# Sparse experts: first layer's bias moved to VectorE, second's bias product over 128 rows, a wait for the expert's own weights, first weights fetched in the layer before

## The chip, the cores and the metric

One core of one Trainium2 chip runs the whole kernel as one program. The metric is the device time of one execution in microseconds (us). "The span" is the time from the first to the last instruction of the profiled execution.

## The reference, cut to what matters

Four layers work on 8 x 512 tokens of width 256, each followed by a normalisation: attention, a quantized two-layer network, linear attention with decay, and at last a latent attention with eight sparse experts. The change is in the last of them:

```python
mla_out = ao @ o_w + o_b
probs = softmax(mla_out @ router_w + router_b)
topw, topi = top_k(probs, 2)
topw = topw / (topw.sum(-1) + 1e-8)
combine = sum(one_hot(topi, 8) * topw[..., None], axis=-2)
h1 = gelu(einsum('bsd,edf->ebsf', mla_out, w1) + b1)   # w1: 8 x 256 x 512
h2 = einsum('ebsf,efd->ebsd', h1, w2) + b2             # w2: 8 x 512 x 256
x = layernorm(hs + hs + 0.3 * einsum('bse,ebsd->bsd', combine, h2))
```

## The kernel before

The program runs one block after another: `attention` ("soft"), `quantized_ffn`, `attention` ("decay"), `latent_attention` ("mla") and `sparse_experts` ("moe"). Within a block the engines have programs of their own, in an order written out by hand, tied by semaphores. SyncE (SP) issues the plain DMAs, GpSimd (POOL) the indirect ones.

**`latent_attention`** scatters each token's vector twice, sorted by expert, into the DRAM tensor `by_expert`, and leaves the number of rows of each expert in `counts`. SyncE first loads weights and small tables, waits for `ones_ready`, and then `spread((0, 0))` copies yh and yl into `stack` and `pad` as soon as they are made. ScalarE writes exponentials into `pt`, four groups deep, one for each t; TensorE reads them in its step "A".

**`sparse_experts`, start.** SyncE issues six small loads (among them `blank`, 1 MB), then 16 weight pieces of 512 KB (w1 and w2 of each expert by turns) through the four buffers of `raw`, a piece from the fifth on only when an older one has been split. VectorE makes `table` (for each of 72 tiles its row in `by_expert` and its expert's number) in 14 steps, out of `counts`. ScalarE makes the high part of each piece (`hi_split`), VectorE the low one (`lo_split`, line 1737). When all pieces are issued, SyncE copies the biases' high and low parts, row by row, 16 DMAs, into `bias` [2, 8, 768], and then `blank` behind the experts' regions in `by_expert` (line 1602). After that it fetches the tiles, line 1612.

**Loop over 72 tiles.** Each tile has 128 rows and one expert. A slot works on four tiles at once. TensorE's order in slot s is: transposes of tile s+2 into `ps_x` (line 1661); first layer of tile s+1 into `ps_h` (a 2-row matmul of `ones` with the bias, line 1670, then six of 512 columns, 1672 to 1674); four transposes of g of tile s (1682); second layer of tile s-1 into `ps_y` (a 2-row bias matmul, 1691, then twelve of 256 columns, 1693 to 1695). ScalarE casts x (1792), makes `g` by Gelu straight from `ps_h` (1798) and casts gh (1804). VectorE makes xl (1743), gl (1747) and the weighted answer yo (1755). GpSimd scatters the answer (1819). Line 1652 loads the expert's number of a tile from `table` into a register of TensorE, once for the first and once for the second layer, since the addresses of the weights depend on it. Before the loop TensorE waits for all 16 splits. Two slots ahead, the first eight tiles and the last ones are written out; 56 slots lie in a hardware loop of seven turns with eight slots each.

**End.** For each of 8 batches SyncE loads the two answers of every token (into `w1h`, four batches deep) and x; GpSimd adds the answers (1825); VectorE adds twice x (1768), takes statistics (1771, 1776) and, a batch later, normalises (1762); GpSimd adds EPS (1832) and takes the power -1/2 (1834). SyncE stores the result.

Of the kernel before, what the change touches and what calls it, by code (L numbers as in the profile page):

```python
# [18 lines left out]
F32 = mybir.dt.float32  # L19
# [6 lines left out]
P = 128  # L26
# [925 lines left out]
def latent_attention(nc, const, x_in, sorted_out, counts, w, name):  # L952
# [8 lines left out]
    with ctx:  # L961
# [27 lines left out]
        pt = sb("pt", [P, TT, 4, SEQ])  # L989
# [108 lines left out]
        with nc.Block() as block:  # L1098

            @block.sync  # L1100
            def _(sp):
# [39 lines left out]
                hold(sp, ones_ready, 2)  # L1141
                spread((0, 0))
# [7 lines left out]
            def _(pe):  # L1150
# [4 lines left out]
                def steps(i, run):  # L1155
                    in_misc = [k for k in run if k in bank]
                    for key in run:
# [43 lines left out]
                        elif kind == "A":  # L1201
# [6 lines left out]
                            for s in range(4):  # L1208
                                last = nc.tensor.matmul(ps_a[32 * s:32 * s + 32, 0, :], v[:, t, 4 * a + s, :], pt[:, t, s, :], start=(t == 0), stop=(t == TT - 1), tile_position=(0, 32 * s))
# [177 lines left out]
            def _(act):  # L1387
# [12 lines left out]
                def steps(i, run):  # L1400
                    for key in run:
# [103 lines left out]
def sparse_experts(nc, const, x_in, by_expert, answers, counts, w, x_out, name):  # L1505
# [6 lines left out]
    with ctx:  # L1512
# [5 lines left out]
        RAW = 4  # L1518
        raw = sb("raw", [P, RAW, KD * F])
        bias = sb("bias", [2, E_, F + D], F32R)  # L1520
        ones = sb("ones", [2, P], F32R)
# [7 lines left out]
        table = sb("table", [P, 2, TILES], I32)  # L1529
# [6 lines left out]
        raw_b = xt[:, :, :].rearrange("p k n -> p (k n)")[0:E_, 0:F + D]  # L1536
        hi_b, lo_b = (x[:, :, :, :].rearrange("p a k n -> p (a k n)")[0:E_, 0:F + D] for x in (gh, gl))
        past = g_line[:, 0:TILES * E_].rearrange("p (n e) -> p n e", e=E_)
        over = g_line[:, TILES * E_:TILES * E_ + E_ * (BATCH * SEQ // P)].rearrange("p (e m) -> p e m", e=E_)
        st6, mv, vare, rstd = sb("st6", [P, 2, TT, 6]), sb("mv", [P, 2, TT, 2]), sb("vare", [P, 2, TT, 1]), sb("rstd", [P, 2, TT, 1])  # L1540
        ps_x, ps_h, ps_g, ps_y = (ctx.enter_context(nc.psum_tensor(f"{name}_{n}", [P, 2, F], F32)) for n in ("ps_x", "ps_h", "ps_g", "ps_y"))
        small_in, staged, hi_split, lo_split = sem("small_in"), [sem(f"staged{k}") for k in range(RAW)], sem("hi_split"), sem("lo_split")
        made, bias_split, bias_in, table_step, counted = sem("made"), sem("bias_split"), sem("bias_in"), sem("table_step"), sem("counted")
# [6 lines left out]
        stored = [sem(f"stored{k}") for k in range(4)]  # L1550
        hold = gated_hold(sem("held"))

        pieces = [(e, n) for e in range(E_) for n in range(2)]
# [6 lines left out]
        x_part = lambda b: raw[:, b % RAW, :]  # L1560
        y_part = lambda b, c: w1h[:, 2 * (b % 4) + c, :, :].rearrange("p k n -> p (k n)").bitcast(F32)
        TABLE = 14
# [21 lines left out]
        with nc.Block() as block:  # L1584

            @block.sync
            def _(sp):
                sp.dma_start(raw_b, w["biases"]).then_inc(small_in, 16)
# [3 lines left out]
                for c, (e, n) in enumerate(pieces):  # L1592
                    if c >= RAW:
                        hold(sp, lo_split, c - RAW + 1)
                    src = (w1, w2)[n][e].rearrange("(k p) n -> p k n", p=P)
                    sp.dma_start(piece(e, n)[0].rearrange("p (k n) -> p k n", n=src.shape[2]), src).then_inc(staged[c % RAW], 16)
                hold(sp, bias_split, 2)
                for e in range(E_):
                    for r, part in enumerate((hi_b, lo_b)):
                        sp.dma_start(bias[r:r + 1, e, :].bitcast(F32), part[e:e + 1, :].bitcast(F32)).then_inc(bias_in, 16)  # L1600
# [24 lines left out]
                for b in range(BATCH):  # L1625
                    if b >= 4:
                        hold(sp, stored[b % 4], 16 * (b // 4))
                    for c in range(2):
                        at = (c * BATCH + b) * SEQ
                        sp.dma_start(y_part(b, c).rearrange("p (t d) -> p t d", d=D), answers[at:at + SEQ, :].rearrange(tok, p=P)).then_inc(tile_in[b % 4], 16)  # L1630
                    if b >= RAW:
                        hold(sp, summed, b - RAW + 1)
                        sp.dma_start(x_part(b).rearrange("p (t d) -> p t d", d=D), x_in[b].rearrange(tok, p=P)).then_inc(staged[b % RAW], 16)
                    if b >= 2:
                        hold(sp, normed, TT * (b - 1))
                        sp.dma_start(x_out[b - 2].rearrange(tok, p=P), y_part(b - 2, 0).rearrange("p (t d) -> p t d", d=D)).then_inc(stored[(b - 2) % 4], 16)
# [293 lines left out]
```

## Time and profile before

| | us |
|---|---|
| median of three runs | 3590.7 (3590.26 to 3591.96) |
| profiled execution, its own time | 3593.07 |
| its span | 3590.8 |
| `latent_attention`, from about | 2366 |
| `sparse_experts`, from about | 3121 |
| first transposes of the loop | 3179.7 |
| first load of the end | 3518.4 |

Over the span TensorE (PE) is busy for 84%, its weight loads (PEld) for 59%, VectorE (DVE) for 56%, ScalarE (ACT) for 38%, GpSimd (POOL) for 26%. The granted TensorE clock is 0.931 of full speed in the mean. Times in the rows are us from the start of the span unless marked ns. "q" behind an engine's name means its sequencer, which loads registers, waits, branches and issues while the engine itself may work or stand; TensorE's sequencer is PEldq.

### The profile page before, as it was taken

The numbers are of one execution on the slowest core, as the hardware profiler recorded it, in microseconds if no ns is written. First come the engines' busy times: TensorE is split into PE (matmuls) and PEld (weight loads), VectorE is DVE, ScalarE is ACT, GpSimd is POOL, SyncE is SP. The second block draws the span as 40 slices with busy tenths as digits, with TensorE's granted clock in tenths as the row PEclk, the third lists the DMA queues.
The fourth block names the chain that finished last, engine by engine and source line by source line (L and its number), as shares of the span: only waits on it lengthen the run. The fifth ranks groups of instructions, "written<-read, shape, count | busy, mean of one in ns | idle before, by whom it ended". The sixth has DMA issues, their size and how long they took to land. (4 is left out here: it accounts for less than half of the span.)

```text
span 3590.8 us, 62854 instructions
## 1 busy us (share of the span) xinstructions
PE 3031.4 (84%) x17666; PEld 2116.8 (59%) x17667; DVE 2019.2 (56%) x3902; ACT 1349.6 (38%) x2815; POOL 941.3 (26%) x1262
## 2 busy tenths in 40 slices
PE   5989898998989985877999999969888888359991
PEld 4665666656666655765777777744444444247771
DVE  3656555465646556764666666556666666333334
ACT  3545445354545441222222222215444444233330
POOL 3332332333333311213333333310111111212224
PEclk8999999999999997997999999979999999679995
DMA  1000000000000002111000000022222222241115
GB/s 46 1 14 1 14 1 14 6 9 14 1 13 1 7 8 73 38 64 58 12 12 12 12 12 12 6 56 59 59 59 59 59 60 57 69 139 58 57 54 171
DMA packets 103470, 132.37 MB, mean 37 GB/s; under 512 B 16472, under 2 KB 80088, under 8 KB 102624
## 3 DMA queue, kind: packets, MB, share of 16 engines
q1 hardware_dynamic: 96352, 110.89, 10.4%
q0 software_dynamic: 6912, 18.96, 1.4%
q8 instruction: 101, 1.65, 0.2%
q14 instruction: 105, 0.86, 0.1%
HBM read 64.66 MB, written 36.78 MB: 28 GB/s over the span
## 5 line engine op out<-in xcount | busy, mean ns | idle before, releaser
L612 ACT ACTIVATE soft_probs<-soft_ps_s,soft_mx 128x512 f32<-128x512 f32 x512 | 348.5, 688 | 359.3 <-DVE soft_mx L516 342.6
L1328 DVE TENSOR_REDUCE mla_mx<-mla_ps_s 128x1 f32<-128x512 f32 x512 | 333.7, 685 | 198.0 <-PE mla_ps_s L1188 195.5
L1430 ACT ACTIVATE mla_pt<-mla_ps_t 128x512 f32<-128x512 f32 x512 | 290.9, 600 | 354.7 <-PE mla_ps_t L1200 349.0
L516 DVE TENSOR_REDUCE soft_mx<-soft_ps_s 128x1 f32<-128x512 f32 x512 | 328.3, 684 | 134.0 <-PE soft_ps_s L405 116.2
L416 PEld LDWEIGHTS soft_ps_p<-ident,soft_probs 128*128 128x128 f32 x2048 | 227.5, 143 | 259.2 <-ACT soft_probs L612 57.5
L416 PE MATMUL soft_ps_p<-ident,soft_probs 128*128 128x128 f32 x2048 | 316.7, 286 | 29.7 <-DVE soft_pt L536 23.1
L405 PE MATMUL soft_ps_s<-soft_ks,soft_qs 128*128 128x512 f32 x1024 | 304.9, 422 | 43.0 <-ACT soft_probs L612 32.2
L434 PE MATMUL soft_ps_m<-soft_pt,soft_v 128*64 128x512 f32 x1024 | 268.3, 610 | 1.3 <-DVE soft_v L505 1.3
L1188 PE MATMUL mla_ps_s<-mla_stack,mla_pad 128*128 128x512 f32 x512 | 229.4, 455 | 26.1 <-DVE mla_mx L1328 21.3
L536 DVE COPY soft_pt<-soft_ps_p 128x512 f32<-128x512 f32 x256 | 174.3, 681 | 104.7 <-PE soft_ps_p L416 103.9
L1200 PE MATMUL mla_ps_t<-mla_shifted,mla_pad 128*128 128x512 f32 x512 | 219.2, 430 | 14.1 <-ACT mla_pt L1430 11.7
L405 PEld LDWEIGHTS soft_ps_s<-soft_ks,soft_qs 128*128 128x128 f32 x1024 | 185.1, 196 | 77.4 <-ACT soft_probs L612 37.2
L407 PE MATMUL decay_ps_s<-decay_qs,decay_ks 128*128 128x512 f32 (+3 forms) x1024 | 195.3, 334 | 31.3 <-DVE decay_pt L523 30.5
L498 DVE TENSOR_TENSOR soft_rt<-soft_ps_m,soft_rope 128x1024 f32<-128x1024 f32 (+1 forms) x96 | 100.4, 1046 | 206.9 <-PE soft_ps_m L110 186.9
L523 DVE TENSOR_TENSOR decay_pt<-decay_ps_s,decay_dec 128x512 f32<-128x512 f32 (+3 forms) x512 | 213.7, 482 | 5.4 <-PE decay_ps_s L407 5.4
L619 ACT COPY soft_pt<-soft_ps_p 128x512 f32<-128x512 f32 x256 | 150.9, 589 | 174.5 <-PE soft_ps_p L416 173.6
L407 PEld LDWEIGHTS decay_ps_s<-decay_qs,decay_ks 128*128 128x128 f32 x1024 | 173.3, 199 | 63.8 <-DVE decay_pt L523 42.3
L649 POOL TENSOR_TENSOR decay_rt<-decay_rt 128x256 f32<-128x256 f32 (+1 forms) x192 | 122.6, 660 | 302.9 <-DVE decay_rt L498 302.9
L649 POOL TENSOR_TENSOR soft_rt<-soft_rt 128x256 f32<-128x256 f32 (+1 forms) x192 | 122.2, 657 | 303.3 <-DVE soft_rt L498 303.3
L1188 PEld LDWEIGHTS mla_ps_s<-mla_stack,mla_pad 128*128 128x128 f32 x512 | 100.8, 197 | 163.5 <-DVE mla_mx L1328 79.9
L498 DVE TENSOR_TENSOR decay_rt<-decay_ps_m,decay_rope 128x1024 f32<-128x1024 f32 (+1 forms) x96 | 100.5, 1047 | 126.0 <-POOL decay_st L654 101.5
L313 ACT CAST decay_st<-decay_rt 128x512 fp32r<-128x512 f32 x64 | 39.7, 620 | 334.1 <-POOL decay_rt L649 220.2
(328 smaller groups left out, 6744.7 us busy)
## 6 DMA issues: line engine op xcount, KB each, us to landing
mla_pad<-mla_stack SPq DMA_DIRECT2D x256, 64.0 KB, 2.0
moe_xt<-by_expert SPq DMA_DIRECT2D x72, 129.0 KB, 2.1
mla_stack<-mla_yh SPq DMA_DIRECT2D x128, 64.0 KB, 2.1
moe_raw<-in_L_ffn_w SPq DMA_DIRECT2D x16, 512.0 KB, 5.1
moe_w1h<-answers SPq DMA_DIRECT2D x16, 512.0 KB, 6.2
soft_xc<-in_L_attn_x SPq DMA_DIRECT2D x8, 512.0 KB, 3.9
x<-soft_r SPq DMA_DIRECT2D x32, 128.0 KB, 2.0
ffn_xc<-x SPq DMA_DIRECT2D x8, 512.0 KB, 3.9
```

Source lines behind the costliest of these rows:

```text
L405: last = nc.tensor.matmul(ps_s[:, t, :], qs[:, h, P * t:P * t + P], ks[:, n, g, :], start=(n == 0), stop=(n == 1))
L407: last = nc.tensor.matmul(ps_s[:, t, P * t:SEQ], ks[:, n, g, P * t:P * t + P], qs[:, h, P * t:SEQ], start=(n == 0), stop=(n == 1))
L416: last = nc.tensor.transpose(ps_p[:, c % 2, P * t:P * t + P], probs[:, h % 2, t, P * c:P * c + P], ident[:, :])
L434: last = nc.tensor.matmul(m[HD * s:HD * s + HD, first_q[c]:SEQ], v[:, 1, c, HD * g:HD * g + HD], weights_of(2 * p + s, c), start=(c == 0), ...
L516: op = vv.tensor_reduce(out=mx[:, h, t:t + 1], in_=ps_s[:, t, :], axis=AX.X, op=ALU.max, negate=True)
L523: op = vv.tensor_tensor(weights_of(h, t), ps_s[:, t, P * t:SEQ], dec[:, h, 0:SEQ - P * t], ALU.mult)
L612: op = nc.scalar.activation(probs[:, h % 2, t, :], ps_s[:, t, :], ACT.Exp, bias=mx[:, h, t:t + 1], scale=1.0, accum_out=rs[:, h, t:t + 1])
L649: op = nc.gpsimd.tensor_tensor(half(0, c), half(0, c), half(1, 1 - c), ALU.add)
L1188: last = nc.tensor.matmul(ps_s[:, (4 * t + s + 16 * a) % S_BANKS, :], pad[:, QUADS + a, s, P * t:P * t + P], stack[:, a, :], start=True, s ...
L1200: last = nc.tensor.matmul(ps_t[:, s % 2, :], pad[:, a, s, P * t:P * t + P], shifted[:, a, :], start=True, stop=True)
L1328: op = vv.tensor_reduce(out=mx[:, a, t, s:s + 1], in_=ps_s[:, (16 * a + 4 * t + s) % S_BANKS, :], axis=AX.X, op=ALU.max, negate=True)
L1430: op = nc.scalar.activation(pt[:, t, s, :], ps_t[:, s % 2, :], ACT.Exp, scale=KPH ** -0.5)
```

## The change

- Line 1670, the first bias matmul, goes. `bias_h` holds b1 of all experts in every partition, by one broadcast DMA of 2 MB. VectorE adds it: `g = ps_h + bias_h[expert]`, with a table load of its own for the expert's number. ScalarE's Gelu then works in place on `g`.
- The second bias matmul stays, but over 128 rows: `ones` is 1 in rows 0 and 1 and 0 elsewhere, `bias_y` [128, 8, 256] is cleared by GpSimd and its two first rows loaded by one DMA out of a DRAM copy `bias_parts`, which two DMAs write.
- TensorE doesn't wait for all 16 splits. Before each first layer it loads a third row of `table`, 2 * expert + 2, and waits until `lo_split` has that value. The table takes 16 steps.
- The first four weight pieces are issued by SyncE in `latent_attention`, between its wait for `ones_ready` and `spread((0, 0))`; `raw` is allocated for both layers, and `pt` has two groups instead of four to make room.
- SyncE's order in the start: small loads, pieces 4 to 7, `blank` into `by_expert`, bias parts, pieces 8 to 11, `bias_y` and `bias_h`, pieces 12 to 15, then the fetches, which wait for these DMAs.
- In the end every batch has buffers of its own in w1h and w1l, so that all loads are issued without a wait; ScalarE normalises, `rstd * y + shift_by`, and issues the stores; GpSimd makes shift_by = -mean * rstd in two more operations.

```diff
-        pt = sb("pt", [P, TT, 4, SEQ])
+        pt = sb("pt", [P, 2, 4, SEQ])
...
                 hold(sp, ones_ready, 2)
+                for dst, src, done in pieces_in:
+                    sp.dma_start(dst, src).then_inc(done, 16)
                 spread((0, 0))
...
                             if s == 0:
-                                act.wait_ge(*(pe_s.at(j, "A", a - 1, t) if a else pe_s.at(shift(j, -1), "A", QUADS - 1, t)))
-                            op = nc.scalar.activation(pt[:, t, s, :], ps_t[:, s % 2, :], ACT.Exp, scale=KPH ** -0.5)
+                                u = 4 * a + t - 2
+                                act.wait_ge(*pe_s.at(j if u >= 0 else shift(j, -1), "A", u % 16 // 4, u % 4))
+                            op = nc.scalar.activation(pt[:, t % 2, s, :], ps_t[:, s % 2, :], ACT.Exp, scale=KPH ** -0.5)
...
# sparse_experts, SyncE
+                for c in range(RAW, RAW + 4):
+                    stage(c)
                 hold(sp, small_in, 16 * 6)
                 sp.dma_start(by_expert[...], w["blank"][1].bitcast(F32)).then_inc(bias_in, 16)
+                hold(sp, bias_split, 2)
+                for r, part in enumerate((hi_b, lo_b)):
+                    sp.dma_start(bias_parts[r], part.bitcast(F32)).then_inc(parts_out, 16)
+                for c in range(RAW + 4, len(pieces)):
+                    stage(c)
+                    if c == RAW + 7:
+                        hold(sp, parts_out, 32)
+                        hold(sp, cleared, 1)
+                        sp.dma_start(bias_y[0:2, :, :].bitcast(F32), bias_parts).then_inc(bias_in, 16)
+                        sp.dma_start(bias_h[:, :, :], w["biases"][:, 0:F].partition_broadcast(P)).then_inc(bias_in, 16)
                 hold(sp, tails_in, 16 * E_)
                 hold(sp, table_step, TABLE)
-                hold(sp, bias_in, 16 * (2 * E_ + 1))
+                hold(sp, bias_in, 48)
...
# TensorE
-                pe.wait_ge(lo_split, len(pieces))
-                pe.wait_ge(bias_in, 16 * 2 * E_)
+                pe.wait_ge(bias_in, 48)
...
                         e = expert_of(i, n)
+                        split = pe.value_load(table[0:1, 2, bass.ds(U * i + n, 1)], min_val=2, max_val=2 * E_)
+                        pe.wait_ge(lo_split, split)
                         pe.wait_ge(xl_done, count(i, n) + 1)
...
-                            pe.wait_ge(g_done, count(i, n) - 1)
+                            pe.wait_ge(h_biased, count(i, n) - 1)
-                        nc.tensor.matmul(m, ones[:, :], bias[:, bass.ds(e, 1), 0:F], start=True, stop=False)
...
-                        nc.tensor.matmul(m, ones[:, :], bias[:, bass.ds(e, 1), F:F + D], start=True, stop=False)
+                        nc.tensor.matmul(m, ones[:, :], bias_y[:, bass.ds(e, 1), :], start=True, stop=False)
...
# VectorE, between xl of tile s+2 and gl of tile s
+                    n = s + 1
+                    if inside(i, n):
+                        e = dve.value_load(table[0:1, 1, bass.ds(U * i + n, 1)], min_val=0, max_val=E_ - 1)
+                        dve.wait_ge(h_done, count(i, n) + 1)
+                        if not isinstance(i, int) or U * i + n >= 2:
+                            dve.wait_ge(back, count(i, n) - 1)
+                        vv.tensor_tensor(g[:, n % 2, :], ps_h[:, n % 2, :], bias_h[:, bass.ds(e, 1), :], ALU.add).then_inc(h_biased, 1)
...
# ScalarE
-                        nc.scalar.activation(g[:, n % 2, :], ps_h[:, n % 2, :], ACT.Gelu).then_inc(g_done, 1)
+                        nc.scalar.activation(g[:, n % 2, :], g[:, n % 2, :], ACT.Gelu).then_inc(g_done, 1)
...
+                for b in range(BATCH):
+                    act.wait_ge(rstd_done, b + 1)
+                    for t in range(TT):
+                        nc.scalar.activation(y_part(b, 0)[:, D * t:D * t + D], y_part(b, 1)[:, D * t:D * t + D], ACT.Identity,
+                                             bias=shift_by[:, b % 2, t, :], scale=rstd[:, b % 2, t, :]).then_inc(normed, 1)
+                    act.wait_ge(normed, TT * (b + 1))
+                    nc.scalar.dma_start(x_out[b].rearrange("(t p) d -> p t d", p=P), y_part(b, 0).rearrange("p (t d) -> p t d", d=D)).then_inc(stored, 16)
...
# GpSimd, for each batch in the end
+                    nc.gpsimd.tensor_tensor(shift_by[:, b % 2, :, :], mv[:, b % 2, :, 0:1], rstd[:, b % 2, :, :], ALU.mult).then_inc(eps_done, 1)
+                    hold(pool, eps_done, 3 * b + 3)
+                    nc.gpsimd.tensor_scalar(shift_by[:, b % 2, :, :], shift_by[:, b % 2, :, :], -1.0, None, ALU.mult).then_inc(rstd_done, 1)
```

## Rows read from the trace of the kernel before

**Rows 1.** Stretches: us, each engine's busy time, granted clock, DMA share, GB/s.

```profile
3121.00:3180.00 59.00, 0.91 (x4) 0.79 (x4) 26.26 (x34) 16.71 (x16) 9.31 (x8) 0.50 0.64 202
3180.00:3515.00 335.00, 333.81 (x1872) 258.42 (x1870) 115.04 (x216) 105.57 (x217) 68.06 (x71) 0.99 0.19 62
3515.00:3590.00 75.00, 0.00 (x0) 0.00 (x0) 39.35 (x105) 0.00 (x0) 35.97 (x25) 0.51 0.62 199
```

**Rows 2.** Timeline of one slot's matmuls: start us, us, instruction.

```profile
3303.59 0.49 PE L1670 MATMUL moe_ps_h<-moe_bias,moe_ones 2*128 x1
...
3304.35 0.40 PE L1673 MATMUL moe_ps_h<-moe_w1l,moe_xh 128*128 x1
3304.58 0.40 PE L1674 MATMUL moe_ps_h<-moe_w1h,moe_xl 128*128 x1
...
3306.05 0.38 PE L1691 MATMUL moe_ps_y<-moe_bias,moe_ones 2*128 x1
...
3306.58 0.28 PE L1694 MATMUL moe_ps_y<-moe_w2l,moe_gh 128*128 x1
...
3307.88 0.38 PE L1661 MATMUL moe_ps_x<-ident,moe_xt 128*128 128x128 f32 x2
```

**Rows 3.** Sequencer by line, same slot: ns min/median/max, first to last start.

```profile
L1652 PEldq TENSOR_LOAD <-moe_table x2: 300/381/462, 3303.3 to 3306.2; - x2
...
L1659 PEldq EVENT_SEMAPHORE  x1: 51/51/51, 3305.3 to 3305.3; - x1
...
L1680 PEldq EVENT_SEMAPHORE  x2: 51/51/51, 3303.2 to 3307.8; - x2
...
L1691 PEldq FUSED_REGOPS  x1: 60/60/60, 3304.1 to 3304.1; - x1
...
L1652 PEldq FUSED_REGOPS  x1: 46/46/46, 3306.1 to 3306.1; - x1
```

**Rows 4.** The same for the slots at 3189.7 to 3193.3.

```profile
L1659 PEldq EVENT_SEMAPHORE  x1: 51/51/51, 3190.9 to 3190.9; - x1
...
L1668 PEldq EVENT_SEMAPHORE  x1: 51/51/51, 3191.7 to 3191.7; - x1
...
L1680 PEldq EVENT_SEMAPHORE  x1: 51/51/51, 3192.4 to 3192.4; - x1
...
L1691 PEldq FUSED_REGOPS  x2: 60/60/60, 3189.8 to 3193.2; - x2
```

**Rows 5.** Groups by line, 3100 to 3591: busy us, mean ns, idle before.

```profile
L1747 DVE TENSOR_TENSOR moe_gl<-moe_ps_g,moe_gh 128x512 fp32r<-128x512 f32 x72 | 49.8, 692 | 163.3 <-ACT moe_gh L1804 163.3
...
L1792 ACT CAST moe_xh<-moe_ps_x 128x256 fp32r<-128x256 f32 x72 | 26.8, 373 | 119.9 <-PE moe_ps_x L1661 119.9
```

**Rows 6.** Timeline of the start.

```profile
3136.84 1.22 DVE L1737 TENSOR_TENSOR moe_w1l<-moe_raw,moe_w1h 128x1024 fp32r<-128x1024 f32 x1
...
3169.15 0.63 SPq L1602 DMA_DIRECT2D by_expert<-in_L_ffn_blank  x1
...
3180.79 0.43 DVE L1743 TENSOR_TENSOR moe_xl<-moe_ps_x,moe_xh 128x256 fp32r<-128x256 f32 x1 [15.60 <-ACT moe_xh L1792]
```

**Rows 7.** Two stretches of the start, columns as in rows 1.

```profile
3137.00:3163.00 26.00, 0.00 (x0) 0.00 (x0) 17.86 (x15) 11.60 (x12) 5.48 (x5) 0.50 0.82 268
3170.00:3176.00 6.00, 0.00 (x0) 0.00 (x0) 0.00 (x0) 0.00 (x0) 0.00 (x0) 0.50 0.71 176
```

**Rows 8.** Timeline of the end.

```profile
3529.97 0.23 POOL L1832 TENSOR_SCALAR moe_vare<-moe_mv 128x4 f32<-128x4 f32 x1
...
3530.38 1.87 POOL L1834 TENSOR_TENSOR moe_rstd<-moe_vare,minus_half 128x4 f32<-128x4 f32 x1 [0.18 <-POOL moe_vare L1832]
...
3559.66 2.34 POOL L1825 TENSOR_TENSOR moe_w1h<-moe_w1h 128x1024 f32<-128x1024 f32 x1 [5.52 <-DMA moe_w1h<-answers]
...
3584.02 1.38 DVE L1762 TENSOR_SCALAR moe_w1h<-moe_w1h,moe_mv,moe_rstd 128x256 f32<-128x256 f32 x4 [1.67 <-POOL moe_rstd L1834]
```

**Rows 9.** SyncE's waits, 2372 to 2390: us in total, times, longest.

```profile
SPq L42 <- ACT mla_yh L1414: 10.7, 1, 10.7
```

More of the change, by code:

```diff
@@ L1208, in steps @@
                             for s in range(4):
-                                last = nc.tensor.matmul(ps_a[32 * s:32 * s + 32, 0, :], v[:, t, 4 * a + s, :], pt[:, t, s, :], start=(t == 0), stop=(t == TT - 1), tile_position=(0, 32 * s))
+                                last = nc.tensor.matmul(ps_a[32 * s:32 * s + 32, 0, :], v[:, t, 4 * a + s, :], pt[:, t % 2, s, :], start=(t == 0), stop=(t == TT - 1), tile_position=(0, 32 * s))
                         elif kind == "BT":
@@ L1502, in _, with piece_load, sparse_experts @@
                 hold(pool, scattered, 128 * BATCH)
-def sparse_experts(nc, const, x_in, by_expert, answers, counts, w, x_out, name):
+RAW = 4
+PIECES = [(e, n) for e in range(E_) for n in range(2)]
+def piece_load(w, raw, e, n):
+    src = w[("w1", "w2")[n]][e].rearrange("(k p) n -> p k n", p=P)
+    return raw[:, (2 * e + n) % RAW, :].rearrange("p (k n) -> p k n", n=src.shape[2]), src
+def sparse_experts(nc, const, x_in, by_expert, answers, bias_parts, counts, raw, staged, w, x_out, name):
     w1, w2 = w["w1"], w["w2"]
@@ L1517, in sparse_experts @@
         w2h, w2l = (sb(n, [P, E_, FT, D], F32R) for n in ("w2h", "w2l"))
[L1518 to L1521, printed above, removed]
+        bias_h, bias_y = sb("bias_h", [P, E_, F]), sb("bias_y", [P, E_, D], F32R)
+        ones = sb("ones", [P, P], F32R)
         every = sb("every", [P, P])
@@ L1549, in sparse_experts @@
             sem("added"), sem("summed"), sem("stats"), sem("means"), sem("eps_done"), sem("rstd_done"), sem("normed"))
-        stored = [sem(f"stored{k}") for k in range(4)]
+        stored, h_biased = sem("stored"), sem("h_biased")
         hold = gated_hold(sem("held"))
-        pieces = [(e, n) for e in range(E_) for n in range(2)]
+        pieces = PIECES
         def piece(e, n):
@@ L1591, in _, with stage @@
                     sp.dma_start(dst, src).then_inc(small_in, 16)
[L1592 to L1600, printed above, removed]
+                def stage(c):
+                    e, n = pieces[c]
+                    hold(sp, lo_split, c - RAW + 1)
+                    sp.dma_start(*piece_load(w, raw, e, n)).then_inc(staged[c % RAW], 16)
+                for c in range(RAW, RAW + 4):
+                    stage(c)
                 hold(sp, small_in, 16 * 6)
                 sp.dma_start(by_expert[E_ * ROOM:E_ * ROOM + E_ * P, :].rearrange("(e p) n -> p e n", p=P), w["blank"][1].bitcast(F32)).then_inc(bias_in, 16)
+                hold(sp, bias_split, 2)
[8 more added lines that the diff above has]
+                        sp.dma_start(bias_h[:, :, :], w["biases"][:, 0:F].partition_broadcast(P)).then_inc(bias_in, 16)
                 hold(sp, tails_in, 16 * E_)
                 hold(sp, table_step, TABLE)
-                hold(sp, bias_in, 16 * (2 * E_ + 1))
+                hold(sp, bias_in, 48)
                 def fetch(i, n):
@@ L1866, in build @@
         attention(nc, const, x2, x3, a["L1_attn_Wq"], a["L1_attn_Wkv"], a["L1_attn_Wo"], None, a["rope1"], a["decay"], False, "decay")
-        latent_attention(nc, const, x3, by_expert, counts, mla, "mla")
-        sparse_experts(nc, const, x3, by_expert, answers, counts, mla, out, "moe")
+        bias_parts = nc.dram_tensor("bias_parts", [2, E_, D], F32, kind="Internal").ap()
+        raw = ctx.enter_context(nc.sbuf_tensor("raw", [P, RAW, KD * 2 * D], F32))
+        staged = [ctx.enter_context(nc.semaphore(f"staged{k}")) for k in range(RAW)]
+        first = [(*piece_load(mla, raw, *PIECES[c]), staged[c]) for c in range(RAW)]
+        latent_attention(nc, const, x3, by_expert, counts, first, mla, "mla")
+        sparse_experts(nc, const, x3, by_expert, answers, bias_parts, counts, raw, staged, mla, out, "moe")
 def tables():
```

79 lines of the change are left out of this document (35 added, 44 removed).

## The prediction

> **What bounds the kernel now.** I read the stages first [rows 1]. The change touches the last two layers' code. Of these, the sparse experts run from 3121 to the end in three stages with different limits: a start (59 us) in which TensorE does 0.9 us of work, a loop over 72 tiles (335 us) in which TensorE is busy 333.8 us at a granted clock of 0.99, and an end (75 us) without any matmul. VectorE is at 115.0/335, a third, in the loop.
>
> Inside the loop the order of the matmuls of one slot shows what TensorE spends [rows 2]. Slot to slot is 4.60 us (335/72 less the ends; the sequencer's wait for g comes at 3303.2 and again at 3307.8 [rows 3]). The first bias matmul to the second full one takes 0.76 us where a full-row 512-column matmul takes 0.23 (3304.35 to 3304.58): the bias costs its own 0.43 and a further 0.1 in the matmul behind it, 0.53 together. The second bias costs 3306.05 to 3306.58 = 0.53 for two 256-column matmuls, where the eleven steps from 3306.58 to the next slot's transposes at 3307.88 give 0.12 each: 0.29 too much. So a 2-row matmul is dear before and behind, not only in itself.
>
> "Busy" TensorE hides a second engine that is nearly full: its own sequencer, which loads the expert's number from the table, checks it, computes addresses and pushes matmuls into a queue [rows 3]. It comes to the wait of the x transposes at 3305.3 and goes on at 3306.1: 0.7 us more than the four pushes need (0.1, below). It goes on when TensorE begins the y bias (3306.05 [rows 2]), so I read this hole as a full queue. It is the sequencer's only slack. In the slots written out by hand just after the start, where it runs free [rows 4], its work is 3190.9 to 3192.4 (x and h, 1.5), to 3193.2 (g and a table load, 0.8), and y 3189.8 to 3190.9 (1.1): 3.4 us. In the loop the parts are 3303.2 to 3304.1 (0.9), y 1.2 with a little stall, and 3306.1 to 3307.8 (1.7, with a load of 0.46 instead of 0.30). Free of stalls that is 0.1 + 0.9 + 1.1 + 1.55, some 3.7, and 3.8 with the loop's branch and its register work (an estimate, a tenth of a us for each slot). So TensorE's sequencer needs 3.8 of the 4.60.
>
> **The change, part by part.**
>
> *First bias off TensorE, second over 128 rows.* TensorE's own slot falls by 0.53 + 0.29 = 0.82 to 3.78 us.
>
> *Own split awaited.* This adds to each slot a second table load on TensorE's sequencer. The block of the first one runs from the x wait at 3190.9 to the wait behind it at 3191.7, 0.8, less the pushes 0.1 [rows 4]; in the loop an address operation of 46 ns and its gap come on top [rows 3]: 0.75. The register-valued wait adds 0.1, the dropped bias saves its address operation and pushes, 0.1. Net +0.75 (bounds: +0.6 without the address operation and with a fast wait, +0.95 with a load of 0.46). Slot on the sequencer: 3.8 + 0.75 = 4.5 us (4.4 to 4.8). That is above TensorE's 3.78, so the sequencer becomes the bound and hands back most of the 0.82. 56 slots lie in the loop: 56 x (4.60 - 4.5) = 6 us. Some 14 full slots outside it have static indices: 3.4 + 0.1 (a further wait of the full slot) + 0.65 = 4.1, so 14 x 0.5 = 7. Together -13 us. What the wait was to bring is nothing: VectorE's and ScalarE's programs still make all 16 splits before their first slot, and h needs xl of VectorE.
>
> The Trainium skill weighs in on this step: "Advanced Engine Details and Errata", section Sequencer Loop, has it that other engine instructions can be read and queued while a control instruction executes. By that the second load would be free and the slot 3.78; the rows contradict it, since pushes stop for the length of a load, and it stands below as a rival.
>
> *The addition on VectorE.* Its nearest row is L1747, the same shape from PSUM and SBUF: 0.69 us [rows 5]. VectorE goes from 1.6 to 2.3 of 4.5 us a slot. It has a table load of its own, hidden: nothing waits on VectorE then but xl, which TensorE takes a slot later. ScalarE's Gelu starts some 0.75 later, but TensorE asks for its result only a slot (4.5 us) after h. If that cover went, each slot would grow by at most 0.75.
>
> *First four weights fetched in the layer before.* Their four issues stand on SyncE in front of `spread((0, 0))`; behind them SyncE waits 10.7 us for yh anyway [rows 9]. The pt tile halves; group u-2 has been multiplied before the matmul of group u that ScalarE waits for (TensorE runs them in order): 0. In the start they save little, since the first split begins only behind the small loads and the table, at 3136.84 [rows 6]. With two more table steps and a smaller bias split they begin as before.
>
> *The start.* Removed: the 16 bias copies that SyncE issues ahead of the blank copy at 3169.15, which then runs alone; the first xl follows at 3180.79 [rows 6]. Added: bias_h, 2.1 MB. Now all is one DMA-bound stretch. From 3137 to 3163 the DMA engines did 0.82 x 26 = 21.3 us at full share, for the 12 last pieces and the tails; the blank is 0.71 x 6 = 4.3, and bias_h at 268/0.82 = 327 GB/s is 6.4 [rows 7]. From 3138 that ends at 3170; with 1 us of gaps, a last cast, split and xl (3 us), xl is at 3174: -7 us. Bounds: -12 if the blank and the tails overlap in idle share, -2 if the broadcast runs at half that rate.
>
> *The end.* All 16 answer loads are issued at once (20 issues with x), stores go to ScalarE's queue, the normalisation to ScalarE. Then GpSimd, in order, sets the pace [rows 8]: add 2.34, add of EPS 0.23, power 1.85, two more small operations of 0.23, four gaps of 0.18: 5.6 us with the add's own gap. The first chain begins at 3530.0 as before, ends 3533.1; six periods of 5.5 end at 3566; the last chain 2.7, four activations of 0.4 (an estimate from L1792, a 128x256 cast of 0.37 [rows 5]), then the 5.4 us that now follow the last normalisation (3584.02 + 1.38 to 3590.8): 3576. -15 us (-9 with GpSimd slowed by VectorE to 6.5, -18 with power at 1.04). The loads do not bind: 10.5 MB at the end's 199/0.62 = 321 GB/s [rows 1] take 33 us from 3518.4 and are done by 3552, ahead of the adds.
>
> Sum: 13 + 7 + 15 = 35 us. Against the profiled execution (3593.1 around a span of 3590.8) this is 3558; against the median 3590.7, 3556.
>
> **Rivals.**
>
> A: the loop is TensorE-bound. If the sequencer's load runs beside the pushes, 72 x 0.82 = 59 us, and 22 from the ends: 3510. For it: there is a queue, and 0.7 us of slack. Against: the slack is smaller than the block. 0.12.
>
> B: the loop gains nothing. Loads of 0.46 instead of 0.30 for two of the three give 4.8 a slot: 72 x 0.2 lost, or TensorE, now idle a fifth, falls to its lower clock at times (in the start it is granted 0.50 after standing still [rows 1]). -22 + 5 to 15: 3572 to 3584. 0.17.
>
> C, the other side: slower. Every table load at 0.5 us, as one kept by traffic: three loads cost 0.6 more, 5.1 a slot, +36 in the loop and -22 outside: 3605. It decides from 4.60 + 29/72 = 5.0 us on. Loads beside a full queue are 0.46; against it, they are 0.30 where the queue is not full, which it will not be. 0.05.
>
> D: the ends do not deliver (GpSimd at 6.5 a batch and the broadcast slow), 11 instead of 22: 3567. 0.05.
>
> **How the numbers follow.** My forecast has 0.61, its own range 3543 to 3568 (loop 13 +- 8, start +-5, end +-5, not all together). A and C lie outside the range, B and D inside: 3536 to 3584, with 0.2 left out. Faster by over 0.2% (7 us, what a measurement of this kernel can tell from none) is the forecast, A, D and nearly all of B: 0.92; within, the edge of B and C: 0.03; slower: 0.05.
>
> **What would show it.** In the profile after: slots of 4.5 us in the loop with TensorE idle 0.7 to 1 us before h; the sequencer's records without the 0.7 us hole, and three loads of 0.30; L1694's matmul 0.12 behind the y bias's; first xl near 3174; 5.5 us from add to add on GpSimd in the end. Slots of 3.8 would show A, 5 us C. I am wrong in kind if the loop is paced by VectorE's addition, or if bias_h lands after 3172.

## The result: 3558.2 us, and the profile after

The changed kernel takes 3558.15 us (median of 4 runs, 3557.32 to 3559.3) against 3591.33 (median of 4 of the kernel before), a ratio of 0.9903 (95% interval 0.9886 to 0.992). The forecast was 3556. The profiled execution took 3557.32 around a span of 3555.5.

The three stages of the experts' layer, cut at the first small load, the first xl and the last matmul's end (windows; us, busy time of each engine, granted clock, DMA share, GB/s; they answer to [rows 1]; the same cuts in the kernel before give 60.0, 333.8 and 76.2, and TensorE is busy for 333.4 of the 333.8):

```profile
3124.50:3175.60 51.10, 1.68 (x6) 1.20 (x6) 26.26 (x38) 17.40 (x19) 11.67 (x9) 0.50 0.78 243
3175.60:3495.50 319.90, 280.10 (x1796) 240.29 (x1796) 151.52 (x288) 106.66 (x215) 67.75 (x71) 0.99 0.20 63
3495.50:3555.50 60.00, 0.00 (x0) 0.00 (x0) 24.25 (x73) 16.59 (x32) 39.11 (x42) 0.53 0.75 249
```

TensorE was busy for all but 0.4 us of the loop; now it stands for 39.8 of 319.9, at an unchanged clock. The timeline of one slot shows where (compare [rows 2]):

```profile
3304.34 0.36 PE L1702 MATMUL moe_ps_y<-moe_bias_y,moe_ones 128*128 x1
3304.55 0.28 PE L1704 MATMUL moe_ps_y<-moe_w2h,moe_gh 128*128 x1
...
3305.97 0.38 PE L1671 MATMUL moe_ps_x<-ident,moe_xt 128*128 128x128 f32 x2
3306.87 0.49 PE L1683 MATMUL moe_ps_h<-moe_w1h,moe_xh 128*128 x1 [0.52 <-issue]
```

It stands once a slot, ahead of the first layer, and what ended it is "issue": the profile shows no semaphore of another engine that it waited for. The groups say the same of the whole layer; the addition on VectorE has the predicted 0.69 us:

```profile
L1683 PE MATMUL moe_ps_h<-moe_w1h,moe_xh 128*128 x144 | 64.9, 451 | 39.5 <-issue 37.9 <-DVE moe_xl L1758 1.3
...
L1765 DVE TENSOR_TENSOR moe_g<-moe_ps_h,moe_bias_h 128x512 f32<-128x512 f32 x72 | 49.8, 692 | 81.8 <-PE moe_ps_h L1685 81.7
```

In the sequencer's records of the same slot (compare [rows 3]) the loads follow at once behind the wait of the x transposes; the hole of 0.7 us is gone, and the three loads take 0.30 to 0.36. The block of the added load, its address operation, load, check and gaps, goes from 3305.8 to the next line's operation at 3306.6 (0.75):

```profile
L1669 PEldq EVENT_SEMAPHORE  x1: 51/51/51, 3304.9 to 3304.9; - x1
```

```profile
L1662 PEldq TENSOR_LOAD <-moe_table x2: 307/334/362, 3305.1 to 3307.4; - x2
```

```profile
L1676 PEldq FUSED_REGOPS  x2: 46/98/151, 3305.8 to 3306.3; - x2
L1676 PEldq TENSOR_LOAD <-moe_table x1: 297/297/297, 3305.9 to 3305.9; - x1
```

```profile
L1678 PEldq ALU_OP  x1: 32/32/32, 3306.6 to 3306.6; - x1
```

The start (timeline; compare [rows 6]): the table is made by 3138.7, the last casts and splits come behind 3169, and xl follows. The fetches wait for bias_h among others and start at 3168.78, so it has landed by then.

```profile
3138.73 1.22 DVE L1752 TENSOR_TENSOR moe_w1l<-raw,moe_w1h 128x1024 fp32r<-128x1024 f32 x1
...
3168.78 2.62 SPq L1632 DMA_DIRECT2D moe_xt<-by_expert  x3
3169.11 1.04 ACT L1800 CAST moe_w1h<-raw 128x1024 fp32r<-128x1024 f32 x1 [5.78 <-DMA raw<-in_L_ffn_w]
...
3175.59 0.75 DVE L1758 TENSOR_TENSOR moe_xl<-moe_ps_x,moe_xh 128x256 fp32r<-128x256 f32 x2
```

The end (timeline; compare [rows 8]): from add to add GpSimd takes 3524.62 - 3519.26 = 5.36 us and does not stand.

```profile
3519.26 2.35 POOL L1848 TENSOR_TENSOR moe_w1h<-moe_w1h,moe_w1l 128x1024 f32<-128x1024 f32 x1
...
3522.10 1.75 POOL L1857 TENSOR_TENSOR moe_rstd<-moe_vare,minus_half 128x4 f32<-128x4 f32 x1 [0.18 <-POOL moe_vare L1855]
...
3524.62 2.35 POOL L1848 TENSOR_TENSOR moe_w1h<-moe_w1h,moe_w1l 128x1024 f32<-128x1024 f32 x1
...
3548.76 2.07 ACT L1825 ACTIVATE moe_w1h<-moe_w1l,moe_shift_by,moe_rstd 128x256 f32<-128x256 f32 x4 [0.46 <-POOL moe_shift_by L1861]
```

### The profile page after: what moved, and what is told of

Same layout as the page of the kernel before. It is cut to its first block and busy times, and to the rows that moved or that the text cites. A ratio compares the mean times of both kernels' runs of the same rounds, so it can differ in the third digit from the quotient of the medians.

```text
span 3555.5 us, 63335 instructions
## 1 busy us (share of the span) xinstructions
PE 2977.8 (84%) x17594; PEld 2096.7 (59%) x17595; DVE 2041.1 (57%) x3946; ACT 1368.9 (38%) x2847; POOL 947.1 (27%) x1279
## 3 DMA queue, kind: packets, MB, share of 16 engines
q10 hardware_dynamic: 4224, 4.19, 0.3%
## 5 line engine op out<-in xcount | busy, mean ns | idle before, releaser
L405 PEld LDWEIGHTS soft_ps_s<-soft_ks,soft_qs 128*128 128x128 f32 x1024 | 185.7, 197 | 76.2 <-ACT soft_probs L612 36.5
```

The source lines that it names most:

```text
L405: last = nc.tensor.matmul(ps_s[:, t, :], qs[:, h, P * t:P * t + P], ks[:, n, g, :], start=(n == 0), stop=(n == 1))
```

## The experiments

The layers ahead of the experts' are the same code in the changed kernel and nearly all experiments, yet the first small load of this layer came at 3114.5 to 3126.4 in the profiles of the first four kernels, which ran together, and at 3161.0 to 3169.8 in those of the next two sets of four, where the kernel before took 3634.14 and 3636.19 instead of 3591.78. The first two sets ran on one chip and the third on another, so the step of some 42 us between the first and the second is not the chip's. Totals are therefore compared within a set only, and the readings rest on the stages, cut as above. "Slot" is the mean distance of 52 successive gl in the middle of the loop.

| kernel | start | loop | slot | end | median | kernel before, same set |
|---|---|---|---|---|---|---|
| before | 60.0 | 333.8 | 4.60 | 76.2 | 3591.33 | |
| changed | 51.1 | 319.9 | 4.48 | 60.0 | 3558.15 | 3591.33 |
| no own split | 51.8 | 267.3 | 3.67 | 60.0 | 3504.84 | 3591.78 |
| load kept, no wait | 52.0 | 319.4 | 4.48 | 60.0 | 3558.83 | 3591.78 |
| before plus a load | 59.4 | 339.0 | 4.61 | 74.2 | 3592.82 | 3591.78 |
| no addition | 51.0 | 315.3 | 4.45 | 60.0 | 3543.51 | 3591.78 |
| first fetch late | 52.6 | 319.7 | 4.48 | 60.3 | 3603.79 | 3634.14 |
| numbers kept | 50.9 | 286.7 | 4.00 | 60.2 | 3569.91 | 3634.14 |
| 2-row y bias | 52.3 | 289.9 | 3.98 | 60.0 | 3569.43 | 3634.14 |
| three additions | 50.0 | 263.7 | 3.61 | 54.7 | 3534.22 | 3634.14 |
| small bias_h | 48.6 | 318.4 | 4.45 | 60.1 | 3598.26 | 3636.19 |
| bias on TensorE | 50.6 | 279.1 | 3.83 | 54.8 | 3549.94 | 3636.19 |
| blank early | 44.1 | 263.9 | 3.61 | 54.8 | 3534.44 | 3636.19 |
| four deep | 51.1 | 319.3 | 4.48 | 65.2 | 3604.01 | 3636.19 |

**No own split.**

```diff
+                pe.wait_ge(lo_split, len(pieces))
                 pe.wait_ge(bias_in, 48)
...
-                        split = pe.value_load(table[0:1, 2, bass.ds(U * i + n, 1)], min_val=2, max_val=2 * E_)
-                        pe.wait_ge(lo_split, split)
```

> The changed kernel without the second table load and without the register-valued wait: TensorE waits once for all 16 splits ahead of its loop. Sequencer theory: the loop's mean slot of 4.48 us loses the load's block (0.30 + 0.15 + 0.02 + 0.05 + four gaps of 0.06 = 0.76) and the wait's address work (0.09), which is 3.63; then TensorE's own 3.78 binds: slots of 3.8 us, 72 x 0.68 = 49 us less, 3509. The start is unchanged, since no slot began before the last split. Rival (the slot of 4.48 is set by a chain over VectorE's addition, not by the sequencer): slots stay above 4.4, 3552 to 3558.

3504.84 us, ratio to the kernel before 0.9758 (0.9742 to 0.9774). The window of its loop:

```profile
3178.00:3445.00 267.00, 264.77 (x1796) 238.72 (x1796) 151.27 (x287) 106.96 (x216) 67.48 (x71) 0.99 0.24 75
```

TensorE is the bound again, and its own slot is not 3.78 but 3.60: that is the distance in most slots, and 3305.59 - 3301.96 = 3.63 from x transposes to x transposes in this one. The slot with the loop's branch takes 4.00, where the changed kernel has 4.84: 0.84 less. The two slots behind it take 3.62 to 3.70.

```profile
3301.96 0.38 PE L1672 MATMUL moe_ps_x<-ident,moe_xt 128*128 128x128 f32 x2
3302.12 0.49 PE L1682 MATMUL moe_ps_h<-moe_w1h,moe_xh 128*128 x1
```

```profile
3305.59 0.38 PE L1672 MATMUL moe_ps_x<-ident,moe_xt 128*128 128x128 f32 x2
```

**Load kept, wait gone.** The edit is the one above, with the `value_load` line left in.

> The changed kernel with the second table load kept and only the register-valued wait gone (one wait for all splits ahead of the loop). Sequencer theory: the load is the cost, the wait only its 0.09 us of address work: slots of 4.39, 3552. Rival (the wait against a register is what costs): slots of 3.8, 3510.

Nothing moves: 3558.83, slots of 4.48, not the 4.39 of my theory. Two windows of 200 us in the loop, the changed kernel's first, have the same TensorE time to 0.1 us. The wait against a register is free; the whole price is the load. Nothing behind this load uses its value here, and it costs as much.

```profile
3200.00:3400.00 200.00, 172.98 (x1125) 148.84 (x1124) 94.21 (x180) 66.13 (x134) 43.17 (x45) 1.00 0.19 60
```

```profile
3200.00:3400.00 200.00, 172.86 (x1123) 148.59 (x1122) 94.57 (x180) 66.50 (x135) 42.51 (x46) 1.00 0.19 60
```

**The kernel before plus a load.**

```diff
                         e = expert_of(i, n)
+                        expert_of(i, n)
                         pe.wait_ge(xl_done, count(i, n) + 1)
```

> The kernel before with the expert's number loaded once more ahead of each first layer, its result unused. Sequencer theory: the slot is the larger of TensorE's 4.60 and the sequencer's 3.8 + 0.71 = 4.5: it stays 4.60 and the time stays 3591 (+- 3); in the records the hole of 0.7 us at the x wait is gone. Rival (a load stops TensorE however full its queue is): slots of 5.3, 3641.

3592.82, ratio 1.0006 (0.9996 to 1.0016): a third load in each slot, which costs the changed kernel 0.8 us of every slot, costs nothing where TensorE needs 4.60. TensorE is busy 199.8 of 200 us although a slot has three loads:

```profile
3200.00:3400.00 200.00, 199.82 (x1125) 154.98 (x1126) 69.49 (x131) 62.69 (x130) 41.99 (x44) 1.00 0.18 58
```

```profile
L1652 PEldq TENSOR_LOAD <-moe_table x3: 298/310/474, 3302.0 to 3304.9; - x3
```

The loop is 5.2 us longer all the same, but hardly by the load. In the 56 slots of the hardware loop it loses 0.4 us (258.2 against 257.8), in the slots with the branch, which go from 4.62 to between 4.62 and 4.86. The other 4.8 us lie in the first slots, where TensorE was granted its full clock 15.0 us behind the first xl, and 5.0 behind it in the kernel before. Windows from 5 to 15 us behind the first xl, the kernel before first:

```profile
3185.80:3195.80 10.00, 10.00 (x52) 7.42 (x51) 3.05 (x6) 3.97 (x10) 0.95 (x1) 1.00 0.70 226
```

```profile
3183.10:3193.10 10.00, 10.00 (x28) 6.62 (x26) 1.45 (x3) 2.92 (x6) 0.00 (x0) 0.50 0.70 223
```

TensorE is busy in all of both, and does 52 matmuls in the one and 28 in the other. Ahead of its first bias matmul it had stood for 0.96 us with the added load, waiting for xl, and for 0.29 in the kernel before; whether that delayed the clock, no run shows.

**No addition.** VectorE's load and addition are left out, TensorE's wait is for g, and Gelu reads PSUM:

```diff
-                        nc.scalar.activation(g[:, n % 2, :], g[:, n % 2, :], ACT.Gelu).then_inc(g_done, 1)
+                        nc.scalar.activation(g[:, n % 2, :], ps_h[:, n % 2, :], ACT.Gelu).then_inc(g_done, 1)
```

> The changed kernel without VectorE's addition and its table load; Gelu reads the first layer's sum itself, so b1 is left out of the result. Sequencer theory: VectorE and ScalarE are hidden, slots stay 4.48, 3558 (+- 3). Rival (the addition lies on the path from h to g): slots fall by up to the addition's 0.69, to 3.8, 3510 or some value between.

The slot goes from 4.48 to 4.45 and the loop is 4.6 us shorter, 2.1 of them in the 56 slots of the hardware loop and most of the rest in the first slots. VectorE's addition is covered: it costs at most 0.03 us a slot. Even that may not be its own, since "small bias_h" below keeps the addition and has slots of 4.45 too. The median, 3543.51, is 15 lower; 10 of these lie ahead of the layer, in code that is not changed (first small load at 3114.5 instead of 3124.5), and are not the addition's.

**First fetch late.** The four early issues go back to the head of this layer:

```diff
# latent_attention
-                for dst, src, done in pieces_in:
-                    sp.dma_start(dst, src).then_inc(done, 16)
# sparse_experts
+                for c in range(RAW):
+                    e, n = pieces[c]
+                    sp.dma_start(*piece_load(w, raw, e, n)).then_inc(staged[c], 16)
                 for c in range(RAW, RAW + 4):
                     stage(c)
```

> The changed kernel with its first four weight pieces fetched by SyncE at the beginning of the experts' start, as before, and not in the layer ahead. My theory: it changes nothing, because the DMA engines stand nearly idle (0.17) from 8 to 16 us after the start's first load while the table is made, and the first split waits for the table: first load to first xl stays 51 us, the whole 3558. Rival (the earlier fetch takes 2.1 MB out of a DMA-bound stretch): 2.1 MB at 327 GB/s, 6.4 us later, 3564.

The start is 52.6 against 51.1; kernels with an unchanged start had 50.9 to 52.3, so at most 1.7 us hang on it, hardly more than that scatter, and not 6.4. In the changed kernel the DMA engines have room while the table is made; with the late fetch they are filled then (windows, the changed kernel's first):

```profile
3130.00:3140.00 10.00, 0.00 (x0) 0.00 (x0) 7.81 (x20) 0.00 (x0) 5.21 (x5) 0.50 0.17 59
```

```profile
3174.00:3184.00 10.00, 0.00 (x0) 0.00 (x0) 6.42 (x17) 4.18 (x4) 4.08 (x4) 0.50 0.73 257
```

**Numbers kept.** The changed kernel, with `kept` a table of registers:

```diff
                         e = expert_of(i, n)
+                        kept[str(i), n] = e
...
-                        e = expert_of(i, n)
+                        e = kept.pop((str(i), n), None)
+                        if e is None:
+                            e = expert_of(i, n)
                         pe.wait_ge(gl_done, count(i, n) + 1)
```

> The changed kernel with its second table load and register wait, but the expert's number of a tile is kept in its register from the first layer's step to the second layer's two slots on, where both lie in one pass of the loop (6 of 8 slots) or outside it; so the third load falls away there. Sequencer theory: each load that goes takes 0.30 + 0.15 + 0.02 and three gaps of 0.06, 0.65, from the slot: 4.42 to 3.77 for six of eight, mean 4.0, 56 x 0.49 + 14 x 0.5 = 34 us less, 3524. Rival (it is the load of the split alone that counts, for what stands behind it): 3558.

Slots of 4.00 and a loop of 286.7, 33.2 less (34 expected): 3.64 to 3.88 where the number was kept, 4.4 where it had to be loaded and in the slot with the branch. A turn of eight slots takes 31.8 us instead of 35.8: 0.66 for each of the six loads that are gone (0.65 expected). It is the count of loads that sets the slot, not which load.

**2-row y bias.** The kernel without own split, with

```diff
-                        nc.tensor.matmul(m, ones[:, :], bias_y[:, bass.ds(e, 1), :], start=True, stop=False)
+                        nc.tensor.matmul(m, ones[0:2, :], bias_y[0:2, bass.ds(e, 1), :], start=True, stop=False)
```

> The kernel without own split (one wait for all splits) and with the second layer's bias product over 2 rows again instead of 128. That slot is bound by TensorE (busy 0.995, 3.60 us). By the prediction's reading of the matmuls a 2-row product costs 0.29 us more: slots of 3.89, 72 x 0.27 = 19 us more, 3524. Rival (the extra time around the 2-row matmuls came from the sequencer's stalls, not from their shape): 3505.

TensorE is busy for 289.1 of 289.9 us, at slots of 3.98: the 2-row matmul costs 3.98 - 3.60 = 0.37 more (3.89 expected). The kernel before has the same slot but for the first bias product, so this one cost 4.60 - 3.98 = 0.63. In the timeline the extra stands before the matmul (0.53 from the g transposes, which gave 0.35 before the 128-row one) and behind it:

```profile
3306.37 0.60 PE L1692 MATMUL moe_ps_g<-ident,moe_g 128*128 128x128 f32 x4
3306.90 0.38 PE L1701 MATMUL moe_ps_y<-moe_bias_y,moe_ones 2*128 x1
3307.20 0.38 PE L1703 MATMUL moe_ps_y<-moe_w2h,moe_gh 128*128 x1
3307.43 0.28 PE L1704 MATMUL moe_ps_y<-moe_w2l,moe_gh 128*128 x1
```

**Three additions** to the kernel without own split: numbers kept as above, and

```diff
# SyncE, behind the small loads (before: behind piece 11)
+                sp.dma_start(bias_h[:, :, :], w["biases"][:, 0:F].partition_broadcast(P)).then_inc(bias_in, 16)
# VectorE, behind bn_aggr of batch b; GpSimd keeps the add of the answers and the power
+                    vv.tensor_scalar(vare[:, b % 2, :, :], mv[:, b % 2, :, 1:2], EPS, None, ALU.add).then_inc(eps_done, 1)
+                    for c in ([b - 1] if b else []) + ([b] if b == BATCH - 1 else []):
+                        dve.wait_ge(powered, c + 1)
+                        vv.scalar_tensor_tensor(out=shift_by[:, c % 2, :, :], in0=mv[:, c % 2, :, 0:1], scalar=-1.0, in1=rstd[:, c % 2, :, :], op0=ALU.mult, op1=ALU.mult).then_inc(rstd_done, 1)
```

> The kernel without own split, and besides: numbers kept in registers as above; bias_h fetched as the first thing behind the small loads; in the end the EPS addition and -mean * rstd (one instruction) on VectorE, so that GpSimd does the addition of the answers and the power alone. Sequencer theory: all slots 3.60, the loop's pass no longer 0.5 longer: -4 us. Start: bias_h falls into the stretch in which the DMA engines are idle: -5. End: GpSimd's period goes from 5.36 to 4.3, but the transfers (10.5 MB in, 4.2 MB out at 321 GB/s: 46 us) then bind: -4. 3492. Rival (start and end are both bound by the sum of their transfers): 3501.

Loop 263.7 (3.6 less than without own split), end 54.7 (5.3 less), start 50.0 (some 2 less, not 5). GpSimd's period in the end is 3506.14 - 3501.62 = 4.52:

```profile
3501.62 2.34 POOL L1857 TENSOR_TENSOR moe_w1h<-moe_w1h,moe_w1l 128x1024 f32<-128x1024 f32 x1
3504.16 2.01 POOL L1864 TENSOR_TENSOR moe_rstd<-moe_vare,minus_half 128x4 f32<-128x4 f32 x1 [0.20 <-DVE moe_vare L1799]
3506.14 2.34 POOL L1857 TENSOR_TENSOR moe_w1h<-moe_w1h,moe_w1l 128x1024 f32<-128x1024 f32 x1
```

The total is 3534.22, a ratio of 0.9726 (0.971 to 0.9742) to the kernel before.

**Small bias_h.**

```diff
-        bias_h = sb("bias_h", [P, E_, F])
+        bias_h = sb("bias_h", [P, 1, F])
...
-                        sp.dma_start(bias_h[:, :, :], w["biases"][:, 0:F].partition_broadcast(P)).then_inc(bias_in, 16)
+                        sp.dma_start(bias_h[:, :, :], w["biases"][0:1, 0:F].partition_broadcast(P)).then_inc(bias_in, 16)
```

> The changed kernel with bias_h of one expert alone (256 KB broadcast instead of 2 MB); VectorE adds expert 0's bias for every tile, so the result lacks the other biases. It sizes the transfer's share of the start, whose first load to first xl took 51.1 us. Theory (the start is bound by the sum of its transfers; in the changed kernel the last third of it runs at 375 GB/s): 1.84 MB less is 4.9 us less, 46.2; loop 320, end 60.0. Rival (the weight pieces are paced by their ring of four buffers, fetch, cast, split, fetch, as the run with bias_h moved to the front suggests, which gained 1 us): 50 or more.

48.6 us, 2.5 less: half of the 4.9 that the transfer alone would take, and neither theory's number. That the other half lies beside the waits of the ring of four buffers is my reading of it; no run shows it.

**Bias on TensorE.** The kernel of three additions, with `bias_y` [128, 8, 768] for both biases, no `bias_h`, no addition, and

```diff
+                        nc.tensor.matmul(m, ones[:, :], bias_y[:, bass.ds(e, 1), 0:F], start=True, stop=False)
```

> The kernel of the run with three additions, but the first layer's bias is a matmul over 128 rows on TensorE instead of an addition on VectorE; bias_h and its 2 MB fall away, Gelu reads PSUM itself. TensorE theory: one 512-column matmul more, 0.23 us: slots of 3.83 instead of 3.60, the loop 72 x 0.23 = 16.6 longer, 280; the start up to 5 shorter, 45 to 50; end 54.7. Rival (any bias matmul costs more than its columns, as the 2-row one did): slots of 4.0 or more.

Slots of 3.83, the loop 15.4 longer: a 128-row bias matmul costs its columns, 0.22. The start is 50.6 although 2 MB fewer are loaded, so at the front bias_h costs nothing.

**Blank early.**

```diff
# build; latent_attention issues it behind the first pieces
+        first.append((by_expert[E_ * ROOM:E_ * ROOM + E_ * P, :].rearrange("(e p) n -> p e n", p=P), mla["blank"][1].bitcast(F32), blank_in))
```

> The kernel of the run with three additions, and the blank copy into by_expert (DRAM to DRAM, 1 MB) is issued in the layer ahead, with the first weight pieces. Theory of the sum: in the kernel before this copy alone held the DMA engines for 4.3 us at full share, so first load to first xl goes from 50.0 to 46; the pieces behind it land sooner, since the slump to 219 GB/s in which it runs is gone. Rival (the copy lies in gaps of the pieces' ring): 49 to 50. Loop 263.7 and end 54.7 as in that run.

The start is 44.1, 5.9 less (4 expected). The layer as a whole takes 362.8 us against 431.0 in the changed kernel and 470.0 before:

```profile
3161.00:3205.10 44.10, 1.68 (x6) 1.21 (x6) 26.24 (x37) 16.70 (x17) 11.68 (x9) 0.50 0.76 255
3205.10:3469.00 263.90, 262.54 (x1797) 238.40 (x1796) 151.55 (x287) 107.31 (x217) 67.19 (x71) 0.99 0.24 77
3469.00:3523.80 54.80, 0.04 (x1) 0.00 (x0) 33.77 (x89) 16.59 (x32) 35.94 (x18) 0.54 0.82 273
```

The blank copy now has a semaphore of its own, `blank_in`, that the fetches wait for. The median is 3534.44 (3525.61 to 3537.06), ratio 0.9721 (0.9701 to 0.9742) to the kernel before; the changed kernel was not run in this set. Against "three additions", run in another set, the totals are too scattered to show the 5.9.

**Four deep.**

```diff
                 for b in range(BATCH):
+                    if b >= 4:
+                        hold(sp, stored[b % 4], 16 * (b // 4))
                     for c in range(2):
```

> The changed kernel, but in the end the loads of batch b wait for the store of batch b - 4, as before, though each batch has its own buffers. Theory (GpSimd's 5.36 us a batch sets the pace, the depth gives nothing): the load of batch 4 may start at 18 us into the end and needs some 5; GpSimd asks for it at 24.6 - 0 = 25 us in: last matmul to end stays 60 (+- 1). Rival (the depth is what brought the 16 us): 65 to 76.

65.2 us: between the two. Batch 4's loads start 3.6 us behind the issue of store 0 (3559.25), and GpSimd stands for 0.71 us before its addition; batch 5's start only at 3571.73, 7.1 behind that of store 1 (3564.62), and GpSimd stands for 4.43. I had priced the load and taken the store as landed at once. The depth is worth 5.2 of the end's 16.2 us.

```profile
3568.55 2.34 POOL L1851 TENSOR_TENSOR moe_w1h<-moe_w1h,moe_w1l 128x1024 f32<-128x1024 f32 x1 [0.71 <-DMA moe_w1l<-answers]
...
3571.73 0.36 SPq L1650 DMA_DIRECT2D moe_w1h<-answers  x1
...
3578.38 2.34 POOL L1851 TENSOR_TENSOR moe_w1h<-moe_w1h,moe_w1l 128x1024 f32<-128x1024 f32 x1 [4.43 <-DMA moe_w1l<-answers]
```

## Why the prediction was right

| term | forecast | measured |
|---|---|---|
| slot in the loop | 4.5 | 4.48 (4.42, and 4.84 with the branch) |
| slots written out | 4.1 | 3.99 to 4.19 |
| loop | -13 | -13.9 |
| start | -7 | -8.9 |
| end | -15 | -16.2 |
| layers ahead | 0 | +3.7 |
| sum of the spans | -35 | -35.3 |

That the total came out to within 0.3 us is in part luck: the three stages gave 39.0 us, 4.0 more than forecast, and 3.7 in the layers ahead took them back. Within the loop the parts came as added up: 7.1 us in the 56 slots of the hardware loop (6 forecast) and 6.8 outside it (7 forecast).

*The bound moved to TensorE's sequencer*: shown. TensorE stands on "issue" (37.9 us); taking one load away frees 52.6 us of loop, taking another in six of eight slots frees 33, and adding one to the kernel before, whose TensorE needs 4.60, costs 0.4 in 56 slots. Rival A, that a load runs beside the pushes, falls in the changed kernel. What the Trainium skill's "Advanced Engine Details and Errata", section Sequencer Loop, says, that other engine instructions can be read and queued while a control instruction executes, the runs do not bear out for a register load on TensorE: in "load kept, wait gone" nothing behind the load needs its value, and it costs 0.8 us a slot. In the kernel before, TensorE stays busy over an added load (199.8 of 200), which I read as matmuls queued ahead of it; where the sequencer is the longer of the two, the loads count.

*Sizes inside the step.* TensorE's own slot was put at 3.78 and is 3.60: I gave the 2-row products 0.53 and 0.29, and they cost 0.63 and 0.37, since I compared only matmuls behind them and not the entry from the transposes. It did not show, because TensorE was not the bound. The register wait's 0.1 is 0. The load's block is 0.75 in the sequencer's records, as forecast, and 0.84 by the slot with the branch; where the 0.09 between them lies, no run shows. One with the other, the slot comes out right.

*The signs.* TensorE stands for 0.52 us before h, not 0.7 to 1; from the start of the x transposes to h it is 0.90 (3305.97 to 3306.87), and 0.16 without own split, so 0.74 more. Behind the y bias the next matmul comes after 0.21 us, not 0.12. The other signs came near enough: slots of 4.48, loads of 0.30 to 0.36, the first xl at 3175.6 in a layer that began 3.7 later, 5.36 from add to add. Two sums of the prediction are off in themselves and change nothing: GpSimd's period adds up to 5.6 where 5.5 was used, and rival B's lower end to 3574 where 3572 was written.

*What the own split brings* was put at nothing: shown, the first xl comes as late with it as without (51.1 and 51.8), and it costs 53 us.

*The addition* is covered: it costs at most 0.03 a slot.

*The first fetch and pt's halves* at 0: the start loses at most 1.7 without the early fetch. The latent layer shows no loss: from its first to its last TensorE instruction it took 720.2 us before and 720.5 after. Of the 3.7 us by which the experts' layer starts later, 3.4 arise ahead of the latent layer, in layers that the change does not touch (the latent layer's first TensorE instruction comes at 2381.0 before and 2384.4 after). In the other profiles, where those layers are the same code, it comes at 2378.3 to 2389.4, so I count it as scatter.

*The start* gave 1.9 more than forecast. It is only partly bound by the sum of its transfers: 1.84 MB less of bias_h gave 2.5 us, 1 MB less of a DRAM-to-DRAM copy 5.9. No run took the other edits of the start back one by one (the 16 bias copies, the order of SyncE), so their shares of the 8.9 are not known.

*The end*: GpSimd's period was put at 5.5 and is 5.36. Loads four batches deep again would bring back 5.2 of the 16.2 us; two thirds of the gain don't come from the depth. That they come from the normalisation's move off VectorE and SyncE's stores out of the loads' queue is argued, from VectorE's busy time in the end (39.7 to 24.3 us), and was not tried by itself.

## What to carry to other kernels

A TensorE that is 100% busy may have a sequencer that is nearly as full behind it (here some 80%, an estimate: 3.8 of 4.60 us a slot). Before matmuls are taken away, add up its register loads, checks and pushes for a pass, and take the larger of the two. A register load per tile cost 0.66 to 0.84 us here once it was no longer hidden, and keeping a loaded number in its register cost nothing; the finer wait took back 52.6 of the 66.5 us that the bias edits had gained in the loop. A bias product of two rows was dear in this stream of 128-row matmuls; padded with zero rows, that of 512 columns cost 0.22 us, what its columns cost in the other matmuls (0.23), and as an addition on VectorE, a third of whose time was taken, at most 0.03. Judge such edits by the stage's own length, since untouched layers scattered by up to 12 us between profiles.

## What the hardware showed that I had not expected

Between 128-row matmuls a product of 2 rows is dearer than the same product over 128 rows with zeros, and by nearly the same amount whatever its columns: with 512 columns 0.63 - 0.22 = 0.41 us, worked out between four kernels, and with 256 columns 0.37, by changing the rows alone ("2-row y bias").

With three additions VectorE's EPS addition of four elements in each partition took 1.30 us, and the last of the eight, with GpSimd at rest, 0.17. The one shown below ended at 3503.98, when GpSimd's addition, begun at 3501.62 with 2.34, ended too (3503.96); VectorE's larger operations that ran beside GpSimd's power kept their 1.23 and 1.41, and the power took 2.01, where the last one, with VectorE at rest, took 1.01. The Trainium skill, "Advanced Engine Details and Errata", section VectorE Performance Modes, has it that VectorE's second SBUF port is shared with GpSimd and that instructions of the two block each other in the two-port modes; the rows agree, down to an operation of four elements; in which mode it ran they do not show.

```profile
3502.68 1.30 DVE L1799 TENSOR_SCALAR moe_vare<-moe_mv 128x4 f32<-128x4 f32 x1
3503.89 0.15 DVE L1802 SCALAR_TENSOR_TENSOR moe_shift_by<-moe_mv,moe_rstd 128x4 f32<-128x4 f32 x1
3504.06 1.23 DVE L1789 SCALAR_TENSOR_TENSOR moe_w1l<-raw,moe_w1h 128x1024 f32<-128x1024 f32 x1
3505.32 1.41 DVE L1792 BATCH_NORM_STATS2 moe_st<-moe_w1l 128x6 f32<-128x256 f32 x4
```

```profile
3526.40 1.01 POOL L1864 TENSOR_TENSOR moe_rstd<-moe_vare,minus_half 128x4 f32<-128x4 f32 x1 [1.39 <-DVE moe_vare L1799]
```

In the second and third set the latent layer took some 40 us longer in every profile (755.8 to 766.9 us from its first to its last TensorE instruction, where the first set and the two kernels had 716.7 to 721.1), with a lower granted TensorE clock. What lowered it, no run shows (windows of that layer, the changed kernel and the one with three additions):

```profile
2368.00:3117.00 749.00, 619.99 (x3056) 343.93 (x3056) 473.97 (x985) 337.53 (x614) 94.16 (x141) 0.90 0.22 60
```

```profile
2368.00:3150.00 782.00, 648.77 (x3056) 364.80 (x3056) 474.56 (x986) 338.85 (x614) 88.23 (x136) 0.87 0.21 57
```
